# An attention and MLP tower on one core: its first fifty microseconds laid out anew

## What is computed

```
def embed(x, kernel, bias, pos_emb):         # kernel: 8 shards of 1575 rows
    acc = 0
    for start, W in shards:                  # a token outside a shard adds the
        acc = acc + W[clip(x - start, 0, 1574)]   # shard's first or last row
    return acc + 8 * bias + pos_emb

h = embed(x, ...)
q, k, v = split(layernorm(h) @ w_qkv.T)      # 32 heads of q, 8 of k and v
a = softmax(causal(q k^T / sqrt(128))) v
h = h + a @ w_dense.T
t = layernorm(h)[:, perm]                    # 16 groups of 64 features
t = gelu(t_group @ up_group) @ down_group    # 64 -> 256 -> 64
out = h + t[:, unperm]
```

## Time and profile before

| | |
|---|---|
| median of 3 runs | 2677.96 us (2677.09 to 2679.35) |
| the profiled execution, its time | 2678.52 us |
| its span | 2676.7 us |
| TensorE busy | 2602.3 us, 97% of the span |
| VectorE, ScalarE, GpSimd busy | 46%, 46%, 34% |
| chain that ended last | 91% on TensorE, 4% VectorE, 3% ScalarE |
| GpSimd's subtraction for one weight tile (L960) | 1299 ns mean |

### The profile page before, as it was taken

How to read it: one execution, slowest core, us unless ns; L and a number is a source line. 1 busy time by engine, 2 the same in 40 slices (tenths; PEclk the granted TensorE clock), 3 DMA queues, 4 the chain that set the end, 5 groups by cost and what they waited for, 6 DMA issues and landing times.

```text
span 2676.7 us, 35616 instructions
## 1 busy us (share of the span) xinstructions
PE 2602.3 (97%) x12864; PEld 2103.9 (79%) x12864; DVE 1244.3 (46%) x3114; ACT 1233.2 (46%) x3054; POOL 906.8 (34%) x726
## 2 busy tenths in 40 slices
PE   5999999999999999999999999999999999999997
PEld 3788888887877777888887777788888777778883
DVE  4444444454544444455454444445545354444443
ACT  3544444445454554445445445544544444444432
POOL 3333333332333333332333333343332333333312
PEclk9999999999999999999999999999999999999998
DMA  4222223322322222432222322252222223222222
GB/s 145 64 68 75 71 72 112 88 73 60 103 79 79 83 72 87 130 81 65 74 88 75 91 82 81 72 137 72 70 82 78 76 87 91 83 72 67 71 72 83
DMA packets 112129, 221.49 MB, mean 83 GB/s; under 512 B 13394, under 2 KB 13394, under 8 KB 111956
## 3 DMA queue, kind: packets, MB, share of 16 engines
q1 hardware_dynamic: 104400, 193.78, 24.4%
q0 software_dynamic: 7424, 25.17, 3.4%
q10 hardware_dynamic: 132, 0.27, 0.0%
HBM read 202.40 MB, written 16.78 MB: 82 GB/s over the span
## 4 chain that ended last, share of the span: by engine, by line
PE 91%; DVE 4%; ACT 3%; issue 1%; DMA 0%; ACTq 0%; POOL 0%; DVEq 0%
PE fb L448 22%; PE fb L450 21%; PE fb L449 21%; PE tp L469 4%; PE sc L448 2%; PE sc L449 2%; PE sc L512 2%; PE sc L450 2%; PE fb L521 2%; PE pv L448 2%; PE pv L450 2%; PE pv L449 2%; ACT w_hi L654 1%; PE sc L460 1%; PE fb L506 1%; PE pv L481 1%
## 5 line engine op out<-in xcount | busy, mean ns | idle before, releaser
L960 POOL TENSOR_TENSOR w_lo<-w_raw,w_hi 128x512 fp32r<-128x512 f32 x640 | 820.6, 1299 | 1605.3 <-ACT w_hi L654 1605.3
L448 PE MATMUL fb<-xn_hi,w_hi 128*128 128x512 f32 x1536 | 609.9, 397 | 3.5 <-DVE stats L859 1.7
L450 PE MATMUL fb<-xn_hi,w_lo 128*128 128x512 f32 x1536 | 600.9, 391 | 0.0
L449 PE MATMUL fb<-xn_lo,w_hi 128*128 128x512 f32 x1536 | 599.6, 390 | 0.0
L654 ACT ACTIVATE w_hi<-w_raw 128x512 fp32r<-128x512 f32 x640 | 382.9, 632 | 383.3 <-PE fb L450 383.3
L448 PE MATMUL fb<-at_hi,w_hi 128*128 128x512 f32 x992 | 394.4, 398 | 8.3 <-DVE hacc L854 6.2
L670 ACT ACTIVATE prob<-sc,neg_max 128x128 f32<-128x128 f32 (+3 forms) x512 | 263.5, 527 | 279.7 <-DVE neg_max L807 273.8
L450 PE MATMUL fb<-at_hi,w_lo 128*128 128x512 f32 x992 | 387.6, 391 | 0.0
L449 PE MATMUL fb<-at_lo,w_hi 128*128 128x512 f32 x992 | 386.9, 390 | 0.0
L448 PEld LDWEIGHTS fb<-xn_hi,w_hi 128*128 128x128 f32 x1536 | 289.1, 188 | 82.1 <-issue 18.8
L450 PEld LDWEIGHTS fb<-xn_hi,w_lo 128*128 128x128 f32 x1536 | 288.8, 188 | 62.1
(11 more groups left out here) (160 smaller groups left out, 3440.2 us busy)
## 6 DMA issues: line engine op xcount, KB each, us to landing
w_raw<-in_w_qkv SPq DMA_DIRECT2D x384, 256.0 KB, 2.7
w_raw<-in_w_dense SPq DMA_DIRECT2D x256, 256.0 KB, 2.7
h_rows<-hacc SPq DMA_DIRECT2D x32, 256.0 KB, 2.3
h_tok<-in_pos SPq DMA_DIRECT2D x12, 512.0 KB, 6.2
mlp_w<-in_w_mlp SPq DMA_DIRECT2D x24, 256.0 KB, 3.0
first_pos<-in_pos SPq DMA_DIRECT2D x4, 512.0 KB, 7.2
end_w<-in_w_mlp SPq DMA_DIRECT2D x8, 256.0 KB, 4.4
hacc<-in_x_row SPq DMA_DIRECT2D x3, 192.0 KB, 8.4
```

What stands on the lines that cost most here:

```text
L448: pe.matmul(dst, a_hi, b_hi, start=first, stop=False)
L449: pe.matmul(dst, a_hi, b_lo, start=False, stop=False)
L450: return pe.matmul(dst, a_lo, b_hi, start=False, stop=last)
L960: pool.tensor_tensor(w_lo[:, m % RW, :], w_raw[:, m % RAW, :], w_hi[:, m % RW, :], ALU.subtract)\
```

## The change

It rewrites the head and touches three things behind it.

- **Edges.** Six DMAs in place of nine, into `mlp_w`'s space, with no wait ahead of them; two float32r halves (64 rows, high and low) made by one copy and one subtraction; the bias is fetched to 18 rows of a 32-row group. `row_buf` isn't zeroed.
- **Coefficients** for one sequence at a time (64x512): for sequence 0 at the start, for the others on VectorE behind step G3 of the sequence before, from token rows that SyncE fetches at step A. The 96x1536 ones at the first K are gone.
- **SyncE** doesn't wait for the edges: positions 0 and 1, two weight tiles, then positions 2 and 3 behind the landing of 0 and 1, two more tiles.
- **Order.** J0 and J1 come first; B, La, Lb, J, X of the chunks are interleaved otherwise.
- **Normalisation** reads the sums' banks, by halves of 512 features (two instructions of 512 columns, each releasing its X). The copies to `h_tok` are steps of their own, C0 to C2 on ScalarE behind the normalisation, C3 on VectorE.
- **First projections** (`ALONE`: Q0, K, Q1, V of unit 0) go to the four banks 2 to 5 of `first_bank` and not to `fb`. Steps a0 to a3 make their columns 0 to 255 ahead of and behind X6 and X7, and Q0, K, Q1, V their columns 256 to 511: 192 products of 256 columns in place of 96 of 512.
- **w0 to w3**: four float32 products, ones by mask, into banks that are free, at the start and between the chunks.
- **Weight tiles** 0 to 10 are split at other steps (`FIRST_SPLITS`).
- **H of sequences 1 to 3** goes to the `pv` bank (`aside`), with its own semaphores, and no more through `fb`; in `MLP0` H0 stands ahead of Y0, Y1 and H1 ahead of Ta0, and the other H steps are spread anew.

```diff
-MLP0 = ("S0 N0 Q2 Y0 Ta0 H0 Y1 Tb0 f H1 S1 H2 E1 N1 Q3 H3 Ta1 D0 Tb1 H4 S2 H5 E2 p F D1 H6 D2 N2 H7 D3 D4 D5 D6 D7 u0 "
+MLP0 = ("S0 N0 Q2 H0 Y0 Y1 H1 Ta0 H2 Tb0 f S1 H3 E1 N1 Q3 H4 Ta1 D0 H5 Tb1 D1 H6 S2 E2 p F D2 H7 D3 N2 D4 D5 D6 D7 u0 "
...
-START = ("A G0 G1 G2 G3 J0 B0 B1 J1 La0 B2 B3 Lb0 J2 La1 X0 X1 Lb1 B4 B5 J3 La2 X2 X3 Lb2 B6 B7 La3 X4 X5 Lb3 X6 X7 "
-         "Q0 K Q1 V VT")
+START = ("A G0 G1 G2 G3 w0 w1 J0 J1 B0 B1 La0 B2 Lb0 B3 La1 J2 X0 X1 w2 Lb1 C0 B4 B5 La2 J3 X2 X3 Lb2 C1 w3 B6 B7 La3 "
+         "X4 X5 Lb3 a0 C2 a1 X6 X7 C3 a2 a3 Q0 K Q1 V VT")
...
+ALONE = (Step("Q", 0, 0, 0), Step("K", 0, 0, 0), Step("Q", 0, 0, 1), Step("V", 0, 0, 0))
...
+FIRST_SPLITS = [Step(k, 0, 0, i) for k, i in (
+    ("B", 1), ("Lb", 0), ("X", 1), ("Lb", 1), ("X", 3), ("Lb", 2), ("X", 5), ("Lb", 3), ("X", 7), ("C", 3), ("Q", 0))]
...
+            first_positions(0)
+            first_positions(1)
+            load(0)
+            load(1)
+            sp.wait_ge(pos_in[0], 16)
+            first_positions(2)
+            sp.wait_ge(pos_in[1], 16)
+            first_positions(3)
+            load(2)
+            load(3)
...
+                    if s in ALONE:
+                        projection(s, product_at(s), S // 2, S).then_inc(alone_full, 1)
+                    else:
+                        projection(s, start_job(s), 0, S).then_inc(job_full, 1)
+                elif s.kind == "a":
+                    if s.i == 0:
+                        pe.wait_ge(*free(Step("X", 0, 0, 3)))
+
+                    pe.wait_ge(first_free, 3 + s.i)
+                    projection(ALONE[s.i], product_at(ALONE[s.i]), 0, S // 2)
+                elif s.kind == "w":
+                    if s.i == 3:
+                        pe.wait_ge(first_free, 1)
+                    pe.matmul(first_bank((0, 1, 5, 6)[s.i]), ones[:, :], mask[:, :], start=True, stop=True)
...
+                if b > 0:
+                    act.activation(normal(b, c), h_tok[:, c, :], ACT.Identity,
+                                   scale=rstd[:, c:c + 1], bias=shift[:, c:c + 1]).then_inc(row_ready, 1)
+                else:
+                    for half in range(2):
+                        act.activation(normal(b, c)[:, half * S:(half + 1) * S], first_bank(2 * c + half), ACT.Identity,
+                                       scale=rstd[:, c:c + 1], bias=shift[:, c:c + 1]).then_inc(row_ready, 1)
...
+                elif s.kind == "C" and s.i < 3:
+                    for half in range(2):
+                        act.activation(h_tok[:, s.i, half * S:(half + 1) * S], first_bank(2 * s.i + half), copy)\
+                           .then_inc(first_free, 1)
...
+            dve.wait_ge(edge_in, 96)
+            dve.tensor_copy(edges[:, :], edge_rows).then_inc(edge_step, 1)
+            dve.wait_ge(edge_step, 2)
+            dve.tensor_tensor(edges[32:64, :], edge_rows[32:64, :], edges[32:64, :], ALU.subtract).then_inc(edge_step, 1)
```

More of the change, by code:

```diff
@@ L168, in __init__ @@
         for m in range(RW):
-            first = Step("B", 0, 0, m) if m < 4 else Step("X", 0, 0, m - 3) if m < 10 else Step("Q", 0, 0, 0)
-            self.splits[first].append(m)
+            self.splits[FIRST_SPLITS[m]].append(m)
         for m in range(RW, len(self.tiles)):
@@ L396, in load, with first_positions, tokens @@
                 sp.dma_start(w_raw[:, m % RAW, :], weights[name][index]).then_inc(w_in[m % RAW], 16)
[L398 to L404, removed]
-            sp.dma_start(xi[:, :], x_cols).then_inc(xi_in, 16)
[L407 to L418, removed]
+            def first_positions(c):
+                sp.dma_start(first_pos[:, c, :], pos[c * P:(c + 1) * P, :]).then_inc(pos_in[c], 16)
+            def tokens(b):
+                for half in range(2):
+                    sp.dma_start(token_row[32 * half:32 * half + 32, :],
+                                 x_row[:, b * S:(b + 1) * S].partition_broadcast(32)).then_inc(x_row_in, 16)
+            sp.dma_start(xi[:, :], x_cols).then_inc(xi_in, 16)
+            for half in range(2):
+                sp.dma_start(edge_consts[32 * half:32 * half + 32, :], edge_cols).then_inc(const_in, 16)
+            tokens(0)
+            first_positions(0)
[8 more added lines that the diff above has]
+            load(3)
+            sp.dma_start(perm[:, :], perm_cols).then_inc(perm_in, 16)
             for s in STEPS:
@@ L423, in _ @@
                     sp.wait_ge(job_full, full(Step("O", s.b - 2, 0, PAIRS - 1) if s.b > 1 else Step("H", 0, 0, 7)))
-                    positions(h_tok)
+                    for c in range(TT):
+                        sp.dma_start(h_tok[:, c, :], pos[c * P:(c + 1) * P, :]).then_inc(pos_in[c], 16)
+                    if s.b > 1:
+                        sp.wait_ge(job_full, full(Step("B", s.b - 1, 0, 7)))
+                    else:
+                        sp.wait_ge(first_full, 2 * TT)
+                    tokens(s.b)
                 if s.kind == "D" and s.g == G - 1:
@@ L450, in product, with projection @@
                 return pe.matmul(dst, a_lo, b_hi, start=False, stop=last)
+            def projection(s, dst, t0, t1):
+                for half in range(2):
+                    m = tally.tile[s] + half
+                    pe.wait_ge(w_ready, m + 1)
+                    for k in range(4):
+                        w = slice(k * P, (k + 1) * P)
+                        mm = product(dst[:, t0:t1], w_hi[:, m % RW, w], w_lo[:, m % RW, w],
+                                     xn_hi[:, 4 * half + k, t0:t1], xn_lo[:, 4 * half + k, t0:t1],
+                                     half + k == 0, half == 1 and k == 3)
+                return mm
             def scores(s):
@@ L584, in _ @@
                         pe.wait_ge(*free(Step("D", s.b, G - 1, 4 * half + 3)))
-                    four(start_job(s), lambda j: hacc[:, 4 * half + j, c * P:(c + 1) * P])
+                    four(s, lambda j: hacc[:, 4 * half + j, c * P:(c + 1) * P])
                 elif s.kind == "Y":
@@ L707, in _ @@
                         act.wait_ge(stored, 128 * s.b)
[L708 removed]
+                    act.wait_ge(*filled(s))
                     act.activation(hacc[:, 4 * half:4 * half + 4, c * P:(c + 1) * P],
[L710 to L711 removed]
+                                   product_at(s).rearrange("p (j t) -> p j t", j=4), copy)\
+                       .then_inc(free(s)[0], 1)
                 elif s.kind == "Y":
```

200 lines of the change are left out of this document (112 added, 88 removed).

## The result

The changed kernel takes 2667.97 us (median of six runs, 2666.3 to 2670.32). The kernel before, run beside it, takes 2677.53 us (six runs, 2674.78 to 2679.35). The ratio is 0.9966, with an interval of 0.9955 to 0.9977. So the direction was right, and the size was wrong: the forecast was 2654.5, and the time is outside its range of 2645 to 2664. The profiled execution took 2666.3 us, with a span of 2664.5, 12.2 less than before. It is the fastest of the six, so the spans fell by more than the medians.

The account below looks back on a forecast made before the run. TensorE was taken as the bound, busy almost everywhere but at the start. Head 23.1 less 0.5 behind V plus 0.9 in MLP0 gave 23.5 us gained: span 2653.2, time 2654.5 us, range 2645 to 2664.

Parts of the forecast that it names:

- Edges: Head, before J0: edges land 3 to 4 us earlier, by 7, with three DMAs fewer; extra bias rows cost nothing.
- T: Start of J0 in the head: taken as 9.8 us, bounds 9 and 12, against 16.3 before; 6.5 us removed.
- gather 0 lands 6.3 later at 9.4: Head, before J0: gather 0 starts 0.6 us earlier, at 3.1, and lands 6.3 us later, at 9.4.
- Rival C: Head: positions and gathers share the DMA engines and land late, J0 at 14, + 4 us: 2659; chance 0.10.
- T to the first shift: Head: B0 starts 1.3 us after T, and the first shift ends 8.1 us after T.
- the rise: Head: TensorE goes from low to high clock level after 5.5 us of unbroken work, 6.7 us after T.
- The loop: Head, between chunks: ScalarE and VectorE in turn take 5.0 us a chunk; shifts at 12.3, 17.2, 22.3 after T.
- a0 to V: First projections: a0 at T + 19.5, 192 products at 0.117 us make 22.5; V done at 52.7, taken at 53.1.
- Behind V: After the first V: weight splits stand ahead of VT's copies on ScalarE; cost 0 to 1 us, taken 0.5.
- MLP0: MLP0, three times: Ta0's wait goes, Y1 waits 1.5 us, hacc waits end; net gain 0.3 us each, 0.9 in all.
- The clock: Head: transposes may not hold TensorE's fast clock; if it therefore falls between the chunks, that is Rival B.
- Rival B: Head loop: TensorE's clock level falls, a0 and a1 run 5.5 us at half pace, + 4 us: 2658; chance 0.10.

Follow-up runs that it names:

- run with three edits: Changed kernel with edges and coef of 96 rows, Ta0 ahead of Y1 in MLP0, and shifts by tensor_scalar: 2653.89 us, ratio 0.9912 to the kernel before.

## Why the prediction was wrong

The measured median is 13.5 us above the forecast one, 2654.5. Of these, 11.3 are in the profiled spans and are taken apart below. The other 2.2 are not the kernel's: I set the median 0.5 below the profiled execution, and here it is 1.7 above it.

**The missing term, 8.45 us.** "Edges" in the change part by part treated a change of shape and type only where it stood in the head (J0's start) and added "the extra bias rows cost nothing that I can see". The same product runs 24 times more in EMBED, three times eight, on the engine that is the bound. Before, it cost nothing to notice, since 96 rows start 0.23 us apart like everything else. Its new cost wasn't in the sum at all, though the trace of before has a row for it. The MLP's first products there have 64 rows and two float32 tensors from SBUF, and start 0.31 us behind a product with 128, where other products are 0.23 apart. This row gives the price of one side only:

```profile
2122.61 0.39 PE L450 MATMUL fb<-xn_hi,w_lo 128*128 128x512 f32 x1
2122.92 1.13 PE L512 MATMUL sc<-y,mlp_w 64*128 64x512 f32 x4
```

With EMBED at 8.5 the forecast would have been 2663.0.

**T, 1.96 us.** The step "gather 0 lands 6.3 later at 9.4" took the landing time from a trace in which gathers had the DMA engines nearly to themselves. I wrote in the next sentences that positions would share them, and gave 12 as the bound, but took 9.8. Measured 11.76 here, 10.23 to 11.71 in other runs with this order of DMAs, 9.37 when the gather goes first. Rival C is this, at half its size.

**T to the first shift: right here, in part by luck.** B0 starts 1.3 behind J0 at the low pace (2.07 us for a pair, 2.08 forecast), the rise comes after some 4 us, and the shift ends 7.9 us behind T for 8.1. But the rise was set at 5.5 us behind B0, and where the low pace lasted longer the same stretch took 9.3 to 9.7 us, in five runs.

**The loop, 2.7 us.** The step "two halves 1.1, ..., the last low part and the shift 0.9: 5.0 us" was mis-sized in two terms, and B in a third.

- A half from PSUM with scale and bias takes 0.78 us, not 0.6. From the first half to the next work of ScalarE it is 1.34 us (31.20 to 32.54) where 1.1 stood, for chunk 1 and again for chunk 2.
- A shift is 1.27 and 1.13 us when GpSimd subtracts beside it, not 0.2. The trace of before had this too: its second shift began just behind a subtraction (34.50).

```profile
34.54 1.23 DVE L911 SCALAR_TENSOR_TENSOR shift<-moments,rstd 128x1 f32<-128x1 f32 x1
```

- The edge product takes 0.43 us for 0.23 here too. It costs 0.4 between the first two shifts (4.45 us apart, 4.07 with 96 rows) and nothing behind them: the second and third are 6.06 apart with either.

The 2.7 us are 1.4 between the ends of the first and second shift, 1.0 to the end of the third and 0.3 to a0. With the 96 rows and the other form of the shift 1.0 is left (12.4 for 11.4), for the most part the normalisation and the J3 that then meets the subtraction. With the shift's form alone 1.2 of 2.0 us came back behind the second shift, as TensorE's B steps were next in line.

**a0 to V, 0.66 us.** 192 products of 256 columns start 0.12 apart, not 0.117, which gives 0.6. ScalarE takes V 0.34 us behind the last product, where 0.4 stood; its split of a tile whose load it waited for (1.22 us) was in the way. The 0.5 of "Behind V" did not come: from the taking of V to VT it is 0.64 us, as before.

**MLP0: the mechanism was right.** A wait of 1.5 for Y1, forecast from rows 11, is 1.41; Ta0's own is gone, Tb0 is 0.5 late, and the waits for `hacc` are gone. The gain is 0.62 each where 0.3 stood, since H in its own bank gave 1.52 and not just those two waits of 0.43.

**The clock: right, and worth more than it was given.** Rival B (the level falls between the chunks) didn't happen: the granted clock is 1.00 from 20 us to V, with and without the mask products, and the pairs take 1.12 us. In the run with whole projections, without a0 to a3, the level falls and costs 3.3 of 9.2 us. The prediction gave the split a value only as order of work.

**Not priced:** 0.25 us once, in the last MLP unit of sequence 1, and a gain of 1.1 us behind the last VT. In that unit TensorE starts two of the MLP's products 0.28 us late, beside a table load of ScalarE that comes late; why it does isn't shown. The 1.1 can't be put down to the change, as the same part varies from -1.1 to +2.6 between runs.

Adding up: 8.45 + 1.96 - 0.2 + 2.7 + 0.66 - 0.5 - 0.96 + 0.25 - 1.1 = 11.3 us, the distance between the forecast span, 2653.2, and the measured one, 2664.5.

## What to carry to other kernels

An edit that changes the shape or type of an operation has to be priced at every place where that operation runs, the repeated ones on the bounding engine first: list its rows by line over the whole span, not only in the stretch that the edit is about, and look in the same trace for another operation of the new shape, for its price. A step moved ahead to fill a wait takes its own waits with it: ask which job had its PSUM bank before, and where in its engine's list the one that frees it stands. And a duration to landing, or of a small operation, holds for the company it was measured in: what else will be on the DMA engines, or on GpSimd, at the new time.

## What the runs showed of the hardware

- A product with 64 rows between products with 128 costs 0.09 us more on each side (0.32 against 0.23 apart), in float32r 0.20 behind it, where its weight load starts with it (501.45) and not beside the product ahead; 96 rows, a third of them zeros, cost nothing.
- A VectorE operation on one column with two SBUF tensors took 1.13 to 1.27 us when it started with a GpSimd subtraction, 0.14 without one, and 0.20 beside one when one tensor is a pointer operand. Where both have much to do, the one that started first kept its time: the addition J3 from 27.00 took its 1.23 us and the subtraction from 27.32 took 2.03 for 1.27; in the run with three edits the subtraction from 25.88 took its 1.27 and J3 from 26.25 took 1.98.
- Gathers took 6.3 us to land before the change, and 8.6 and 9.6 (medians, two runs of the changed kernel) beside the positions and weights.
- Behind the first B step TensorE stayed at the low pace for 4 us in one run and for 12 in another of nearly the same kernel, and the granted clock's record doesn't show the whole of it: it read 1.00 while pairs of products took 2.07 us.
